# Windowed attention with a mixture of experts: three product buffers, two planes of boundary probabilities, and value products ahead of the transposes

## The reference, cut to what matters

```python
c1, scale = 16, 16 ** -0.5
qkv = xt @ w_qkv.T + b_qkv            # 1600 pixels x 384
q, k, v = split(qkv)                  # q * scale, 8 heads
k_w, v_w = windows(k), windows(v)     # unfolded, then read anew as (17*17, heads, 16)
attn = softmax(einsum('bhnc,bhnlc->bhnl', q, k_w))
attn = attn * mask_w                  # zero outside of the image
out = einsum('bhnl,bhnlc->bhnc', attn, v_w) @ w_proj.T + b_proj
x = x + out
t = t + moe(layernorm(t))             # router, top 2 of 8, gelu between two matmuls
```

## Time and profile before

| what | value |
| --- | --- |
| median of 3 runs | 486.2 us (483.1 to 486.77) |
| profiled execution | 487.27 us |
| its span, first to last instruction | 485.3 us |
| granted clock of PE, mean | 0.896 of full |
| PE busy | 434.1 us (89%) |
| DVE busy | 339.4 us (70%) |
| ACT busy | 269.4 us (56%) |
| POOL busy | 194.3 us (40%) |

### The profile page before, as it was taken

The page is one execution under the profiler, slowest core; times in us unless marked ns, Lnnn a source line. Parts: engine busy times, 40 slices in busy tenths (PEclk is TensorE's granted clock), DMA queues, the critical chain, the costliest instruction groups (busy, mean ns, idle before and its releaser), DMA issues.

```text
span 485.3 us, 16662 instructions
## 1 busy us (share of the span) xinstructions
PE 434.1 (89%) x6962; PEld 302.0 (62%) x6962; DVE 339.4 (70%) x837; ACT 269.4 (56%) x489; POOL 194.3 (40%) x249
## 2 busy tenths in 40 slices
PE   4899938679789998999999999997699999999996
PEld 2689925447557776776666777665455555865553
DVE  1241174659999999999998899994487554274553
ACT  2240085776879998999999996873000000361332
POOL 9403045175656664666677675751300000000110
PEclk9785568979999999999999999999799756789999
DMA  6069995855545766566665654469740000007400
GB/s 197 18 214 296 217 299 166 277 170 183 193 158 170 235 206 197 182 222 190 215 214 187 210 191 155 157 180 235 259 92 0 1 0 0 1 0 266 162 17 34
DMA packets 39480, 77.24 MB, mean 159 GB/s; under 512 B 9412, under 2 KB 26453, under 8 KB 38589
## 3 DMA queue, kind: packets, MB, share of 16 engines
q1 hardware_dynamic: 38542, 74.61, 49.1%
q0 software_dynamic: 144, 1.36, 0.8%
q10 hardware_dynamic: 720, 0.22, 0.2%
HBM read 45.76 MB, written 29.29 MB: 155 GB/s over the span
## 4 chain that ended last, share of the span: by engine, by line
PE 54%; DVE 27%; issue 9%; DMA 4%; ACT 3%; SPq 2%; DVEq 0%; POOL 0%; POOLq 0%; ACTq 0%
PE ps L878 11%; DVE slabs L1052 10%; PE ps L804 7%; DVE pm L1090 4%; PE ps L917 4%; PE ps L769 4%; PE ps L937 3%; PE ps L827 3%; DVE scn L1062 3%; DVE sbd L1037 3%; DMA zsl<-uv 3%; PE ps L849 3%; PE ps L762 3%; DVE ebd L1086 3%; PE ps L809 2%
## 5 line engine op out<-in xcount | busy, mean ns | idle before, releaser
L804 PE MATMUL ps<-slabs 128*32 128x401 f32 x528 | 119.2, 517 | 17.5 <-POOL slabs L529 8.9
L804 PE MATMUL ps<-prb,slabs 128*32 128x401 f32 x494 | 115.2, 520 | 0.0
L1052 DVE COPY_PREDICATED slabs<-con,zt 128x1152 f32<-128x1152 int32 x41 | 80.5, 1963 | 0.1
L667 ACT ACTIVATE exb<-scn,lowest 128x401 f32<-128x401 f32 x120 | 74.1, 621 | 9.2 <-DVE lowest L1062 9.2
L1062 DVE CUSTOM_DVE_ANT_0 scn<-ps,con 128x401 f32<-128x401 f32 x120 | 63.7, 570 | 20.7 <-PE ps L809 20.4
L809 PEld LDWEIGHTS ps<-con,slabs 128*32 128x32 f32 x960 | 42.4, 113 | 49.8 <-issue 49.4
L809 PE MATMUL ps<-con,slabs 128*32 128x128 f32 x960 | 61.4, 278 | 0.7 <-issue 0.7
L576 POOL TENSOR_TENSOR xln<-xln,wide 128x400 f32<-128x400 f32 x4 | 4.9, 1228 | 134.6 <-DVE wide L1229 134.6
L827 PE MATMUL ps<-con,exb 128*128 128x128 f32 x360 | 48.7, 278 | 10.5 <-DVE pm L1090 10.0
L656 ACT ACTIVATE prb<-slabs 64x1169 f32<-64x1169 f32 x40 | 47.2, 1179 | 19.4 <-DVE slabs L1052 18.5
L522 POOL TENSOR_TENSOR slabs<-con,qrot 128x192 f32<-128x192 f32 (+4 forms) x67 | 30.8, 462 | 64.1 <-DVE slabs L1052 56.2
(11 more groups left out here) (141 smaller groups left out, 767.9 us busy)
## 6 DMA issues: line engine op xcount, KB each, us to landing
slabs<-zsl SPq DMA_DIRECT2D x40, 539.5 KB, 4.2
zsl<-uv SPq DMA_DIRECT2D x44, 484.5 KB, 4.1
slabs<-combd SPq DMA_DIRECT2D x2, 1600.0 KB, 9.0
skb<-zsl SPq DMA_DIRECT2D x4, 539.5 KB, 7.5
slabs<-kimd SPq DMA_DIRECT2D x2, 881.7 KB, 12.4
vimd<-vimg SPq DMA_DIRECT2D x1, 1612.0 KB, 6.0
xt<-x_in SPq DMA_DIRECT2D x8, 200.0 KB, 7.4
frd<-wide SPq DMA_DIRECT2D x2, 800.0 KB, 6.0
```

The costliest lines, as they stand in the source:

```text
L667: nc.scalar.activation(v(ex[x & 1], a, (1, NC3)), v(scn, (x & 1) * NB * NC3 + a, (1, NC3)), ACT.Exp, scale=-1.0, bias=lowest[:, NB * (x & ...
L804: mm(bank(g, (1, NC3), parts=TW, p0=TW * i), w, v((kt, kh)[b & 1][x & 1], b // 2 * C, (1, NC3)), start=first, stop=False, skip_group_check ...
L1052: last = nc.vector.copy_predicated(v(kt[x & 1], 0, (C, NU), (1, C)), cv(name, (9, NU), (1, C), off=(1 - C - ph) % K).bitcast(I32), v(zt, a ...
```

## The change

- The boundary products get three buffers instead of two; a product waits for the sum of three columns before, and for the product before it.
- POOL's order in an iteration becomes spread, mask, `boundary_mul(i+3)`, `boundary(i+1)`. Ahead of the loop, the product of column 2 comes before the injection of column 0.
- DVE no longer adds the two halves of the boundary probabilities. It writes them into two planes of `ebs`, and PE's permutation adds them by accumulation: eight matmuls instead of four.
- On PE the value products of column i-2 come ahead of the transposes of column i-1.
- `skb` shares its place with the second plane, so the value image's second part and the expert weights move to a q buffer, and SP waits for the last product before it loads the former.

```diff
-        xt, xln = sb("xt", L), sb("xln", NCC * XE)
-        qrot, sbd, ebd = sb("qrot", SZ * YP), sb("sbd", SZ * YP), sb("ebd", L)
+        xt, xln = sb("xt", 3 * NCC * SZ), sb("xln", NCC * XE)
+        qrot, sbd = sb("qrot", SZ * YP), sb("sbd", SZ * YP)
+        ebs = sb("ebs", L + 2 * NU * C)
+        ebd, skb = ebs[:, 0:L], ebs[:, L:L + 2 * NU * C]
...
-        kprod = [xt[:, i * NCC * SZ:(i + 1) * NCC * SZ] for i in range(2)]
+        kprod = [xt[:, i * NCC * SZ:(i + 1) * NCC * SZ] for i in range(3)]
...
-        gv, gv_own = zt, skb
+        gv, gv_own = zt, qb[1]
...
-        w1s, w2s = sk
+        w1s, w2s = [qb[1][:, i * E8 * C:(i + 1) * E8 * C] for i in range(2)]
...
-                    sp.wait_ge(S["zt_ready"], 3 * NZK)
+                    sp.wait_ge(S["kmul"], SZ)
                     images_in(sp, vimd, gv, gv_own, S["vim_in"])
...
             def boundary_mul(x):
                 c, xi = divmod(x, XC)
                 pool.wait_ge(q_in[c & 1], 16 * NCC * (c // 2 + 1))
-                pool.wait_ge(S["kadd"], x - 1)
+                if x >= 3:
+                    pool.wait_ge(S["kadd"], x - 2)
+                pool.wait_ge(S["kmul"], x)
...
+            boundary_mul(2)
             boundary(0)
-            boundary_mul(2)
             boundary(1)
...
                 if 2 <= i + 1 < SZ:
                     spread(i + 1)
-                    boundary(i + 1)
                 if 2 <= i < SZ and not inner(i):
                     mask(i)
                 if i + 3 < SZ:
                     boundary_mul(i + 3)
+                if 2 <= i + 1 < SZ:
+                    boundary(i + 1)
...
+                if 0 <= i - 2 < SZ:
+                    products(i - 2)
                 if 0 <= i - 1 < SZ:
                     turn_probs(i - 1)
-                if 0 <= i - 2 < SZ:
-                    products(i - 2)
...
-                mm(bank(k, (1, Q)), cv("perm"), ebd[:, k * Q:(k + 1) * Q], start=True, stop=True
-                   ).then_inc(S["eb_perm"], 1)
+                for p in range(2):
+                    last = mm(bank(k, (1, Q)), cv("perm"), v(ebs, p * L + k * Q, (1, Q)), start=(p == 0), stop=(p == 1))
+                last.then_inc(S["eb_perm"], 1)
...
                 p_ = pm[x & 1]
-                if x >= 1:
-                    dve.wait_ge(S["eb_red"], x)
-                tt(pb[:], bank(7, (64, 2), (1, SZ), off=128 + 8), mask(4 * SZ, (1, 2 * SZ)), ALU.mult).then_inc(S["pb_masked"], 1)
+                tt(v(ebs, x, (L, 2), (SZ, SZ)), bank(7, (64, 2), (1, SZ), off=128 + 8), mask(4 * SZ, (SZ, 2), (1, SZ)),
+                   ALU.mult).then_inc(S["eb_red"], 1)
...
-                dve.wait_ge(S["pb_masked"], x + 1)
-                tt(v(ebd, x, (SZ, SZ)), v(pb, 0, (1, SZ)), v(pb, SZ, (1, SZ)), ALU.add).then_inc(S["eb_red"], 1)
```

More of the change, by code:

```diff
@@ L207, in program @@
         uv = [sb(f"uv{i}", SLAB) for i in range(2)]
-        skb = sb("skb", 2 * NU * C)
         sk = [skb[:, i * NU * C:(i + 1) * NU * C] for i in range(2)]
@@ L222, in program @@
         mx = [sb(f"mx{i}", 6 * SZ) for i in range(2)]
-        pb = sb("pb", 2 * SZ)
         osel = sb("osel", NPS * SZ)
@@ L265, in program @@
             qhalf_in slab_copied w_ready inj_ready kt_half kt_turned scores_done shifted exps pt_done mask_ready masked inner_out
-            kh_zero kh_copied pb_masked eb_red av_done o_used fd_ready
+            kh_zero kh_copied eb_red av_done o_used fd_ready
             eb_perm vprod vacc rot_out nat_in zsum rden rexp_ready r_nat att_nat proj_done
@@ L541, in boundary_mul @@
                 pool.wait_ge(q_in[c & 1], 16 * NCC * (c // 2 + 1))
-                pool.wait_ge(S["kadd"], x - 1)
+                if x >= 3:
+                    pool.wait_ge(S["kadd"], x - 2)
+                pool.wait_ge(S["kmul"], x)
                 n = 8 * NCC
-                gp.tensor_tensor(v(kprod[x & 1], 0, (1, NCC), (NCC, SZ), parts=n),
+                gp.tensor_tensor(v(kprod[x % 3], 0, (1, NCC), (NCC, SZ), parts=n),
                                  v(qb[c & 1], xi * SZ, (XE, NCC), (1, SZ), parts=n),
@@ L1036, in boundary_add @@
                 n = 8 * NCC
-                nc.vector.tensor_reduce(v(sbd, x * YP + 7, (1, SZ), parts=n), v(kprod[x & 1], 0, (NCC, SZ), (1, NCC), parts=n),
+                nc.vector.tensor_reduce(v(sbd, x * YP + 7, (1, SZ), parts=n), v(kprod[x % 3], 0, (NCC, SZ), (1, NCC), parts=n),
                                         AX, ALU.add).then_inc(S["kadd"], 1)
```

## The result

The changed kernel takes **494.7 us** (median of 4 runs, 494.21 to 497.25), against 486.15 us for the kernel before on the same chip: ratio 1.0191, 95% interval 1.0149 to 1.0233. It is slower by 1.9%; the forecast was 484.0 us, and 494.7 lies above the range. The span of the profiled execution is 492.9 us, 7.6 more than before.

The account below looks back on a forecast made before the run. DVE was taken to set the pace up to column 26, with PE and ACT close behind on inner columns, then PE. Terms 4.3 - 5.0 - 3.2 - 1.9 + 0 + 2.9 = -2.9 us gave 484.0 us, range 479.5 to 491.5.

Parts of the forecast that it names:

- PE's order: On PE, value products ahead of transposes: both wait for the same masks, so PE's wait is neither longer nor shorter.
- POOL's order: In the loop, the product fills POOL's wait ahead of the injection: DVE's turn saves 1.1 us per front edge column.
- columns 4 to 10: Front edge columns: 34.1 us against 39.1, at DVE's 5.68 us a column; gain 5.0 (bounds 3 and 5.3).
- one piece of 4.3 us: POOL's spread, injection, mask and product in an edge column run together in 4.3 us, just fitting between DVE's turns.
- Columns 10 to 26: Inner columns: ACT's floor of 5.83 us comes next, 94.1 us in all; gain 3.2 (bounds 1.1 and 5).
- The start: Up to column 4: column 2's injection comes behind a product waiting for q's second chunk; loss 4.3 us (bounds 3.5, 5.6).
- The end: Column 39's scores to last value products: chain 13.5 us without gaps, 18.6 with both; 0 net (bounds -3.8 and +1.4).
- the low clock within the loop: Sign of a wrong forecast: PE at its low clock within the loop, which no step foresees.
- The permutation: Behind the loop: permuting the boundary probabilities takes eight matmuls instead of four, with nothing to hide them; loss 2.9 us.
- planes: Boundary halves on DVE: the separate addition goes, the remaining product writes with a stride; net gain 0.31 us a column.
- POOL doesn't fit: Rival: POOL's sequence passes 4.3 us, blocking the turn by up to 1.0 us and delaying the injection; 491 us, chance 0.13.
- the turn stays long: Rival: DVE's turn stays at 2 us or more, another POOL operation taking the product's place; 492.7 us, chance 0.09.

Follow-up runs that it names:

- kernel 2: The changed kernel with PE's old order (transposes ahead of value products): 483.75 us, 0.989 of the kernel before.
- kernel 5: The changed kernel with PE's old order and value-slab stores and reloads cut to 16 of 128 partitions from column 4 on (output differs): 477.92 us, one run.
- kernel 7: Kernel 6 with POOL's mask moved behind its product and ahead of the injection: 481.26 us, 0.9905 of the kernel before.
- kernel 8: Kernel 7 without the planes: DVE adds the boundary halves again, the permutation is four matmuls; 479.83 us, 0.9896 of the kernel before.
- 6: Kernel 2 with the injection of column 2 ahead of the product of column 4 in POOL's iteration 1: 482.25 us, 0.9918 of the kernel before.
- kernel 9: The changed kernel with DVE's pick one step earlier, between the turn and the weighting: 491.9 us, 1.0134 of the kernel before.
- 10: Kernel 7 with PE's new order and DVE's pick moved ahead of the weighting: 487.44 us, 0.9964 of the kernel before.

## Why the prediction was wrong

**The step that failed is "PE's order"**: "both wait for the same masks, so PE's wait is neither longer nor shorter". The value products wait for one thing more than the masks, DVE's pick of the column before, and that semaphore stands in the printed code. Without the order the changed kernel takes 483.75 us against the forecast of 484.0 (0.989 of before would be 480.8), inside the range. That it comes so near is partly luck: against the terms of the sum kernel 2 is 3.0 us worse in columns 4 to 39 and 2.7 better at the end and the permutation. The order is the whole distance to 494.7, 8.6 us by the spans, 10.9 by the medians and 14.6 by the ratios. By stage against kernel 2 it costs 2.1 us in columns 4 to 10, where it ties PE to DVE's pace and two gaps (2.1 us) open, 4.9 in 10 to 26, where eight more open, 0.7 in 26 to 39, 2.9 at the end and 0.8 at the permutation. The waits for the pick, 5.2 us in the changed kernel, could be foreseen from the code; the gaps could not.

**POOL's order: the mechanism right, smaller in the edge columns.** Without PE's order columns 4 to 10 took 36.22 us and, with the mask moved, 35.38; predicted were 34.1, which kernel 5 reached (34.18) with light transfers. So 2.0 of the 2.1 us that kernel 2 lacks go with the slabs' traffic. A part of it is one wait, which the timelines of POOL and PE of kernel 2 show:

```profile
120.53 1.48 POOL L546 TENSOR_TENSOR xt<-xln,wide 120x600 f32<-120x600 f32 x1 [0.78 <-DMA xln<-qd]
121.97 2.29 POOL L529 TENSOR_TENSOR slabs<-con,sbd 128x384 f32<-128x384 f32 x1
```
```profile
124.52 0.50 PE L807 MATMUL ps<-slabs 128*32 128x401 f32 x1 [1.28 <-POOL slabs L529]
```

The chunk is late, the injection comes behind the turn that began at 121.67 and takes 2.29 us, and PE waits 1.28. In kernel 5 the chunk was 0.22 us late, the injection began ahead of the turn, and PE didn't wait. The forecast's one piece of 4.3 us overlooked the wait for the chunk and the mask's wait for the weighting of an earlier edge column; moving the mask was worth little.

**Columns 10 to 26** came to 94.85 us without PE's order, against 94.1 predicted; **26 to 39** to 82.03 against 81.9. ACT's floor of 5.83 in the inner columns held.

**The start** was right: POOL waits for the chunk ahead of the injection of column 2, +4.2 us in kernel 2, for 4.3, and +3.1 in the changed kernel, below its bound of 3.5, since the chunk landed 1.5 us earlier there.

**The end** was priced too low. Upper bound +1.4, measured +2.0, though only one gap came (2.91), not two. The chain is the one worked out: 2.06 us of waiting at 344.24 and 350.83 are the weighting and the pick, for 1.64 + 0.3. Without the gaps the chain was priced at 13.5 us and took 16.3. What was mis-sized is PE's own work in it, priced at the full clock; 0.3 more is the pick, counted once and paid twice. Behind the gap of 2.91 us, in which PE stood still, the windows from 337 to 341 and from 345 to 351 us show the granted clock at 0.57 and 0.77, the low clock within the loop that the forecast named as a sign that it was wrong:

```profile
337.00:341.00 4.00, 2.90 (x65) 2.88 (x66) 0.00 (x0) 1.03 (x2) 0.00 (x0) 0.57 0.91 205
...
345.00:351.00 6.00, 3.94 (x97) 3.60 (x99) 2.10 (x8) 0.00 (x0) 1.08 (x1) 0.77 0.62 171
```

The products at 344.24 take 1.79 us until the next start instead of 1.12, and DVE starts 2.8 us after the next transposes do, for 2.1.

**The permutation** was priced right at 2.9; the changed kernel paid 1.9 only because its clock stood at 0.87 there against 0.65 before. The **planes** were expected to be worth 0.31 us a column. That holds for DVE's own time (L1080 takes 0.29 us above and replaces 0.24 and 0.50), but with POOL out of the way DVE isn't what ends last, and columns 4 to 26 gained 1.1 us (kernel 7 against 8) for 2.7 to 5.1 paid behind the loop.

Of the **rivals** none was the cause; a trace of the first is the wait of 1.28 us in kernel 2. "POOL doesn't fit" (491) and "the turn stays long" (492.7) gave nearly the time, by another mechanism: turns are 1622 ns long on average here and 1631 in kernel 2, which is 11 us faster. A version to keep is kernel 8: third buffer, POOL's order with the injection of column 2 first and the mask behind the product, no planes, PE's old order, at 0.9896 of before. Kernels 2, 6 and 7 (0.989, 0.9918, 0.9905) can't be told from it, so the runs' times don't show what the early injection, the late mask or the missing planes add to PE's old order; the stages alone do.

**Left open:** why the new order has ten gaps in PE's issue in columns 4 to 26 and the old one five. What was shown is that they are waits for instruction packets and need the DMA traffic, not why the position of the value products decides. The order alone doesn't: the kernel before has two gaps where kernel 2 has five, and of the new order kernels 9 and 10 have three and one where the changed one has ten. These three kernels wait for other engines in the stretch (7.7 us for DVE in the kernel before, 6.7 and 3.3 for POOL in 9 and 10, from behind column 4 to column 26), so a reading that fits is that a wait elsewhere gives the instructions time to arrive. No run tests it.

## What to carry to other kernels

Before two steps of an in-order engine change places, list every semaphore that each of them waits for, and find for each what work stood between its release and the wait: the pick had 1.7 us of transposes as cover in the old order and none in the new one. When an edit relieves the engine that sets the pace, its neighbours at 95% allow only a small gain, and a second edit that helps the same engine (the planes, the mask) is worth its price only where that engine still ends last. Time such bundles edit by edit: here one part lost more than the others together gained.

## What the runs showed of the hardware

An engine can stand still because its instructions arrive late. Every one of the 75 gaps in PE's issue in these traces ends 1.2 to 1.7 us after the end of a 16 KB instruction packet. They depended on other traffic: columns 10 to 26 of the changed kernel had 5.0 us of them with full slab transfers, and none with 16 of 128 partitions moved; and on the program, with 2.2 us in PE's old order and none in kernel 9, where PE waited 5.9 us for POOL.

An instruction of POOL can be the one that stands still. The injection took 1.03 us at 95.63 in the changed kernel and 2.23 at 196.29 in kernel 9, where it began half a microsecond after a turn of DVE (195.75, 1.90 us long). The Trainium skill, page SBUF — State Buffer, section Who interferes with whom, says that such a pair exclude each other for a whole instruction; here the rows agree in both directions, 2.61 instead of 1.48 us for the turn and 2.23 instead of 1.03 for the injection.
